# Where the second layer's block sums are added, who folds them, and when the next tile's steps are issued, in a DLRM tower with a cross network on one core

## The reference, cut to what matters

```python
# e: (512 samples, 39 fields, 16 dims), gathered from 39 tables by ids
x0 = xk = e
for W in (f0, f1, f2):               # (39*39,128), (128*39,128), (128*39,128)
    z = einsum('bfd,bgd->bfgd', x0, xk).reshape(b, f * g, d)
    cur = einsum('bpd,pm->bmd', z, W)          # (512, 128, 16)
    outs.append(cur); xk = cur
z = sum(concatenate(outs, axis=1), axis=-1)    # (512, 384)
h = relu(concatenate([z, dense_ctx], axis=1) @ W_top1 + b_top1)
h = relu(h @ W_top2 + b_top2)
y = h @ W_top3                                 # (512, 1)
```

## Time and profile before

| | us |
|---|---|
| median of 3 runs | 809.71 (808.66 to 812.67) |
| the profiled execution | 812.4 |
| its span | 810.6 |
| PE busy | 738.8 (91%) |
| DVE busy | 677.0 (84%) |
| POOL busy | 488.3 (60%) |
| ACT busy | 285.4 (35%) |

### The profile page before, as it was taken

One profiled execution on the slowest core, in us unless ns is written; L12 is line 12 of the kernel. 1 busy time (PEld: TensorE's weight loads), 2 busy tenths in 40 slices (PEclk: granted clock), 3 DMA queues, 4 the chain that ended last, 5 costly groups with the idle time before them and its releaser, 6 DMA issues.

```text
span 810.6 us, 11627 instructions
## 1 busy us (share of the span) xinstructions
PE 738.8 (91%) x3392; PEld 581.3 (72%) x3392; DVE 677.0 (84%) x2218; ACT 285.4 (35%) x792; POOL 488.3 (60%) x512
## 2 busy tenths in 40 slices
...
DMA packets 12961, 11.16 MB, mean 14 GB/s; under 512 B 3938, under 2 KB 11842, under 8 KB 12644
## 3 DMA queue, kind: packets, MB, share of 16 engines
...
HBM read 10.40 MB, written 0.00 MB: 13 GB/s over the span
## 4 chain that ended last, share of the span: by engine, by line
PE 47%; DVE 34%; POOL 8%; issue 7%; ACT 2%; DMA 1%; SPq 0%; POOLq 0%; DVEq 0%; ACTq 0%
DVE acc L642 23%; PE y L797 8%; PE y L799 7%; PE y L798 7%; PE side L815 5%; DVE z L608 4%; POOL z_parts L350 3%; PE y L863 3%; PE acc L779 3%; PE rep L764 2%; DVE diag L650 2%; POOL sum L365 2%; PE acc L773 2%; DVE acc L639 2%; PE side L804 2%
## 5 line engine op out<-in xcount | busy, mean ns | idle before, releaser
L642 DVE SCALAR_TENSOR_TENSOR acc<-y,x_rows,acc 128x128 f32<-128x128 f32 x1856 | 503.7, 340 | 77.0 <-PE y L799 76.6
L797 PE MATMUL y<-w_hi,x_parts 128*128 128x512 f32 (+1 forms) x640 | 272.9, 426 | 2.3 <-DVE x_parts L614 1.5
L799 PE MATMUL y<-w_hi,x_parts 128*128 128x512 f32 (+1 forms) x640 | 249.9, 391 | 0.0
L798 PE MATMUL y<-w_lo,x_parts 128*128 128x512 f32 (+1 forms) x640 | 249.6, 390 | 0.0
L467 ACT ACTIVATE scaled<-y,x_rows 128x128 f32<-128x128 f32 x512 | 145.9, 368 | 245.6 <-PE y L799 244.9
L350 POOL TENSOR_TENSOR z_parts<-z,z_parts 128x512 fp32r<-128x512 f32 x109 | 140.8, 1292 | 64.8 <-ACT z_parts L413 64.6
L340 POOL DMA_INDIRECT emb<-in_tbl_dram,ids_sb x142 | 143.7, 1012 | 32.8 <-issue 21.1
L797 PEld LDWEIGHTS y<-w_hi,x_parts 128*128 128x128 f32 x640 | 121.1, 189 | 35.9 <-DVE acc L642 8.4
L799 PEld LDWEIGHTS y<-w_hi,x_parts 128*128 128x128 f32 x640 | 120.9, 189 | 25.4
L798 PEld LDWEIGHTS y<-w_lo,x_parts 128*128 128x128 f32 x640 | 121.4, 190 | 24.2
L413 ACT ACTIVATE z_parts<-z 128x512 fp32r<-128x512 f32 x112 | 70.7, 633 | 191.4 <-DVE z L608 191.3
...
## 6 DMA issues: line engine op xcount, KB each, us to landing
...
emb<-in_tbl_dram,ids_sb POOLq DMA_INDIRECT x142, 2.4
...
```

What stands on the lines that cost most here:

```text
L642: dve.scalar_tensor_tensor(part, term, x0_f, part, ALU.mult, ALU.add).then_inc(terms_in, 1)
L797: pe.matmul(dst, x1_hi[:, t % 2, cols], hi, start=True, stop=False)
L798: pe.matmul(dst, x1_hi[:, t % 2, cols], lo, start=False, stop=False)
L799: pe.matmul(dst, x1_lo[:, t % 2, cols], hi, start=False, stop=True).then_inc(y_ready, 1)
```

## The change

- `BY_ACT` goes from (1, 5) to (0, 5). The accumulators `acc` are gone: DVE adds banks 1 to 4 in place on the slice of `scaled` that ACT wrote from bank 0, and banks 6 to 9 on the slice from bank 5. The first bank after one of ACT's waits for `y_act`; term i of a later bank waits for term i of the bank before. All 31 terms of DVE are now `scalar_tensor_tensor`.
- POOL's four steps of a block become three (512 wide, 256 wide, 128 wide), all after DVE's last term, placed at `j == 2` of the next block behind that slot's `low_part`.
- Layer 1 of the next tile starts earlier: chunks at slots 4c (`B_AT` 0), `contract` at 8 + 4c, x1's split at 34 and 35; the tile's first replication and its copy go to slots 34 and 35 of the tile before (tile 1's ahead of the main loop).
- All that hangs on `side` moves two slots later: `S_LAG` 18, columns at 10, 13, 20, 23, rows at 30, 33, layer 3 at 9 to 17, the top network at 20 to 31.

```diff
-BY_ACT = (1, 5)
-A_AT = 0
-B_AT = 3
+BY_ACT = (0, 5)
+FINISH_AT = 2
+A_AT = 34
+B_AT = 0
-CONTRACT_LAG = 7
-X1_AT = 35
-S_LAG = 16
+CONTRACT_LAG = 8
+X1_AT = 34
+S_LAG = 18
...
-T_AT = (8, 11, 18, 21)
-R_AT = (28, 31)
+T_AT = (10, 13, 20, 23)
+R_AT = (30, 33)
...
-L3_AT = 7
+L3_AT = 9
-H1_AT = 18
-H2_AT = 23
-Y_AT = 29
+H1_AT = 20
+H2_AT = 25
+Y_AT = 31
...
-            def fold_scaled(k):
-
-                pool.wait_ge(y_act, act_banks(BANKS * k + BANKS - 1))
+            def finish_x2(k):
+
+                pool.wait_ge(terms_in, dve_terms(BANKS * k + BANKS - 1))
                 pool.tensor_tensor(sum4[:, :], scaled[:, k % 2, 0, :], scaled[:, k % 2, 1, :],
                                    ALU.add).then_inc(four_in, 1)
                 pool.wait_ge(four_in, k + 1)
                 pool.tensor_tensor(sum2[:, :], sum4[:, 0:2 * M], sum4[:, 2 * M:4 * M], ALU.add).then_inc(two_in, 1)
-
-            def finish_x2(k):
-
-                pool.wait_ge(terms_in, dve_terms(BANKS * k + BANKS - 1))
-                pool.wait_ge(two_in, 2 * k + 1)
-                pool.tensor_tensor(sum2[:, :], sum2[:, :], acc[:, k % 2, :, :].rearrange("p a m -> p (a m)"),
-                                   ALU.add).then_inc(two_in, 1)
...
-                    if j == BY_ACT[-1] + 1:
-                        fold_scaled(k)
-                    if j == 0 and k > 0:
-                        finish_x2(k - 1)
...
+                    if j == FINISH_AT and k > 0:
+                        finish_x2(k - 1)
...
+                h = sum(1 for a in BY_ACT if a < j) - 1
+                if j == BY_ACT[h] + 1:
+                    dve.wait_ge(y_act, act_banks(n - 1))
                 for i, f in enumerate(fields_of(j)):
...
+                    part = scaled[:, k % 2, h, i * M:(i + 1) * M]
+                    if j > BY_ACT[h] + 1:
+                        dve.wait_ge(terms_in, first + i - FPB + 1)
+                    dve.scalar_tensor_tensor(part, y2[n % RING][:, i * M:(i + 1) * M], x0_f, part,
+                                             ALU.mult, ALU.add).then_inc(terms_in, 1)
```

More of the change, by code:

```diff
@@ L526, in _ @@
             x1_high(0)
+            three(1)
             for t in range(TILES):
@@ L532, in _ @@
                         scale_bank(n)
+                    if t + 2 < TILES and s == A_AT + 1:
+                        three(t + 2)
                     if t + 1 < TILES:
-                        if s == A_AT + 1:
-                            three(t + 1)
                         c = s - HIGH_LAG - B_AT
@@ L629, in add_bank @@
                 dve.wait_ge(y_ready, n + 1)
-                if j == 0 and k >= 2:
-                    dve.wait_ge(x2_in, k - 1)
                 first = dve_terms(n) - len(fields_of(j))
-                in_block = first - dve_terms(BANKS * k) + len(fields_of(0))
+                h = sum(1 for a in BY_ACT if a < j) - 1
+                if j == BY_ACT[h] + 1:
+                    dve.wait_ge(y_act, act_banks(n - 1))
                 for i, f in enumerate(fields_of(j)):
                     x0_f = x0_rows[:, t // TPG % 2, k % (TPG * NBLK), f:f + 1]
-                    part = acc[:, k % 2, (in_block + i) % 2, :]
-                    term = y2[n % RING][:, i * M:(i + 1) * M]
-                    if in_block + i < 2:
-                        dve.tensor_scalar(part, term, x0_f, None, ALU.mult).then_inc(terms_in, 1)
-                    else:
-                        dve.wait_ge(terms_in, first + i - 1)
-                        dve.scalar_tensor_tensor(part, term, x0_f, part, ALU.mult, ALU.add).then_inc(terms_in, 1)
+                    part = scaled[:, k % 2, h, i * M:(i + 1) * M]
[3 more added lines that the diff above has]
+                                             ALU.mult, ALU.add).then_inc(terms_in, 1)
             def spread_rows(t, half):
@@ L892, in _ @@
                     rest_columns_t(c - 1)
+            pe.wait_ge(prod, C0)
+            pe.wait_ge(cols_lo, prepared(0))
+            pe.wait_ge(cols_hi, prepared(0))
+            replicate(1, -1)
             pe.wait_ge(w1_hi_in, len(W1_CUTS) - 1)
```

16 lines of the change are left out of this document (7 added, 9 removed).

## The result

The changed kernel takes 820.59 us (median of 4 runs, 816.88 to 821.57) against 810.02 us (808.66 to 812.67, 4 runs) of the kernel before: a ratio of 1.011, 95% interval 1.0086 to 1.0134. It is 1.1% slower, where 806.7 us (799 to 815) had been forecast. The profiled execution took 821.57 us, its span is 819.8.

A forecast was written before the change was run, and what follows sets the result against it. VectorE was taken as the bound in ordinary tiles. Terms +6.3 - 4.1 - 3.3 - 4.0 + 0.8 + 1.35 = -3.0 us took the median of 809.7 to 806.7 us, range 799 to 815.

The forecast's parts named there:

- VectorE's own work, nothing saved: VectorE's terms: replacing 128 plain multiplications by scalar_tensor_tensor costs 0, as both start about 0.26 us apart.
- The 8.5 us that the prediction estimated beside its sum: VectorE's 128 replaced multiplications: possible loss if the skill's perf-mode table held; 0 was used in the sum.
- The new wait for ScalarE: Ordinary tiles: VectorE stalls 0.84 us at slot 16, 0.39 at 21, 0.1 to 0.2 at 31; +6.3 over seven tiles.
- Tiles 0 and 1: First two tiles: GpSimd loses one 256-wide step a block, its queue stops growing, both tiles take 40.5 us; -4.1 us.
- Tiles 4, 8 and 12: Tiles with layer 3 and the top network on TensorE: 55.5 us, -1.1 us each, -3.3 in all.
- Tiles 2, 6 and 10: Tiles with column copies through side: 48.2 us against 49.5, -1.3 each, -4.0 in all before 0.8 for the clock.
- 0.8 us for the clock: Tiles 2, 6 and 10: added for TensorE's clock falling in one tile in two more, after the slot 23 pause.
- The tail: Behind VectorE's last term: GpSimd does three steps instead of two, +1.35 us fully on the path.
- The slower one: Rival: ScalarE becomes the bound in tiles 2, 4, 6, 8, 10, 12, 2.6 us each, 822 us; chance 0.18.

The follow-up runs named there:

- e2: The changed kernel with HIGH_LAG 3 instead of 2, so ScalarE scales bank 15 before it rounds chunk 3: 811.78 us, ratio 0.9996 to the kernel before.
- e10: The changed kernel with only the second diag of each tile moved, from slot 12 to 25: 807.13 us, ratio 0.9947 to the kernel before.
- e1: The changed kernel with diag in slots 5 and 25 instead of 2 and 12: 804.23 us, ratio 0.9911 to the kernel before.
- e6: The kernel before (old accumulators and fold) with the new times and diag in slots 5 and 25: 808.27 us, ratio 0.9781 to the kernel before.
- e4: The kernel before (old accumulators and fold) with only the new times and the first replication moved up: 817.81 us, ratio 1.0069 to the kernel before.

## Why the prediction was wrong, point by point

- **VectorE's own work, nothing saved: right** for the terms. The eight from 220.98 on take 2.16 us, so one starts every (2.16 - 0.34) / 7 = 0.26. The 8.5 us that the prediction estimated beside its sum didn't come, as its own row had said: the plain multiplications of before were spaced 0.26 us already.
- **The new wait for ScalarE: right.** 0.84, 0.40 and 0.28 us against 0.84, 0.39 and 0.1 to 0.2; no wait at slot 36; the tile 40.5 against 40.4. Over the seven ordinary tiles +6.7 us, against +6.3. e2 shows that ScalarE's order is the cause.
- **Tiles 0 and 1: -2.9 us instead of -4.1.** The queue of GpSimd stopped growing as said, and tile 1 has the 40.5 of the forecast. Tile 0 has 42.0: its first `diag` took 1.77.
- **Tiles 4, 8 and 12: -0.4 each instead of -1.1.** The waits were right: `s_block` of slot 18 waits 0.83 us for layer 3's copy (0.9 said), as TensorE's row in tile 4 of the kernel after shows, and the one behind the top network's copy is gone. The difference is not the blocked `diag`, since e10 has 56.2 without it. It lies in the terms of the sum: TensorE reaches slot 9 after 7.6 us (7.8 said), takes 36.1 from there to bank 29 (35.8 said), and 12.5 from there to the next tile (11.9 said). That e1 has 55.4, with 55.5 said, is luck: it is 0.8 us from the first `diag`'s new place, which the forecast didn't have.

```profile
271.05 0.81 PE L794 MATMUL side<-diag,x_sb 128*128 128x320 f32 x2 [0.83 <-ACT r_sb L404]
```

- **Tiles 2, 6 and 10: +4.8 us in all instead of -3.2.** This is two thirds of the error. A `diag` of 2.57, 2.55 and 1.37 us stands ahead of a column copy, and in tile 2 the low clock follows. The forecast had 0.8 us for the clock, half of a fall of 1.6 at slot 23; there it came once, in tile 2, and cost 1.6 (e10: 49.7 with it, 48.1 without). The fall at the longer pause of slot 12 cost 2.7 more (tile 2 of e2, which has that one alone, 53.3, against 50.6 in tile 6 of the kernel after) and was in no term. Without either and without the collision e10 has 48.1, against 48.2 said: the chain of waits was right.
- **The tail: right**, +1.35. Another 0.5 us came from the stages behind it, whose length goes with the clock: e1, with the same pause of 5.65 us, has 27.6 us there instead of 30.2.
- **The rivals.** The slower one named the right side for the wrong reason: ScalarE's order costs in tiles 4, 8 and 12 the 1.1 us that e2 takes off, by the wait just shown, and not 2.6 in each of six tiles.

**The step that failed** is the one that put GpSimd's meetings with VectorE at nothing, in "POOL, tiles 0 and 1" and in "Tiles 2, 6 and 10": GpSimd's fold was costed by its length and its place in GpSimd's queue, and nothing was said of what VectorE does at that moment. The forecast took each VectorE duration from the trace of before as if it belonged to the instruction. It belongs to a schedule in which, by its order, no `diag` had met a GpSimd tensor instruction with more than 0.09 us left. In the kernel after such meetings cost about 10 of the 12 us between forecast and measurement; with the one in slot 12 moved away (e10) the ratio is 0.9947, and the forecast's is 0.9963. That the two are so close is in part luck, since tiles 4, 8 and 12 are above their forecast and the time behind the last term is below it. Another 2 us is the mis-sized sum of tiles 4, 8 and 12. The changed order was there to be read: both in slots 2 and 12. No row of before has a price for it, so the right forecast would have had a rival with a range: from 0 to about 1.3 us (the fold's length) for each of 32, 0 to some 40 us, all of it on the slower side. (The longest excess measured, with a gather under way, was 1.76.)

**What stays open.** In tile 6 `diag` was issued 0.59 us ahead of the fold (354.54 and 355.13) and still lost to it; in e6 a `diag` issued 0.62 us ahead of one took 0.81, and in e4 one issued 0.59 us ahead of a low part (tile 1) took 0.81 too. In e2, tile 2 has a `diag` 0.58 us ahead that took 2.54, and tile 6 one 0.61 us ahead that took 0.82. A gather was running at the start of all five. So the order of issue alone doesn't decide who is blocked, and the runs don't show what does. And why TensorE's clock fell behind 3.1 us of pause in tile 2 and not in tile 6 isn't shown either.
